# Scan of a Mamba layer: C rows through DRAM in fp32, C products shared by VectorE and GpSimd, one drive tile scaled on VectorE

## The reference, cut to what matters

```python
x_dbl = einsum('bld,ed->ble', silu(conv(x)), x_proj_w)   # 8 + 16 + 16 rows
dt = softplus(x_dbl[..., :8] @ dt_proj_w.T + dt_proj_b)
Bm, Cm = x_dbl[..., 8:24], x_dbl[..., 24:]
def step(h, inputs):                                     # over the tokens
    dA = exp(dt_t[..., None] * A)
    h = h * dA + (dt_t * x_t)[..., None] * B_t[:, None, :]
    y = einsum('bds,bs->bd', h, C_t)
y = (ys + D * x) * silu(z)
```

## Time and profile before

| | |
|---|---|
| device time, median of 3 runs | 2769.23 us (2762.33 to 2771.55) |
| profiled execution, span | 2740.5 us |
| profiled execution, own time | shown only as its span |
| VectorE busy | 2446.6 us, 89% |
| TensorE busy | 2368.5 us, 86% |
| ScalarE busy | 2302.2 us, 84% |
| GpSimd busy | 1461.6 us, 53% |
| DMA mean | 40 GB/s |

### The profile page before, as it was taken

One profiled execution on the slowest core, in us unless ns is written; L12 is line 12 of the kernel. 1 busy time (PEld: TensorE's weight loads), 2 busy tenths in 40 slices (PEclk: granted clock), 3 DMA queues, 4 the chain that ended last, 5 costly groups with the idle time before them and its releaser, 6 DMA issues.

```text
span 2740.5 us, 93631 instructions
## 1 busy us (share of the span) xinstructions
PE 2368.5 (86%) x38272; PEld 1254.1 (46%) x38289; DVE 2446.6 (89%) x3408; ACT 2302.2 (84%) x4212; POOL 1461.6 (53%) x2897
## 2 busy tenths in 40 slices
...
GB/s 137 1 0 1 23 77 113 63 49 62 34 39 29 49 54 42 31 37 48 48 43 26 49 43 53 36 33 49 34 56 32 42 47 33 40 29 11 2 1 16
DMA packets 47022, 110.41 MB, mean 40 GB/s; under 512 B 5250, under 2 KB 39938, under 8 KB 42306
## 3 DMA queue, kind: packets, MB, share of 16 engines
...
## 4 chain that ended last, share of the span: by engine, by line
PE 36%; issue 17%; DVE 12%; ACT 12%; POOL 11%; DMA 1%; ACTq 0%; DVEq 0%; SPq 0%; POOLq 0%
PE bank L709 11%; PE bank L778 11%; PE bank L789 9%; ACT E L1052 9%; DVE NM L1430 8%; POOL acc L1668 2%; POOL H L1678 1%; ACT acc L1003 1%; POOL H L1681 1%; POOL smp L1661 1%; PE bank L690 1%; POOL dg L1726 1%; PE bank L703 1%; ACT UB L1014 1%; POOL H L1684 1%
## 5 line engine op out<-in xcount | busy, mean ns | idle before, releaser
L1430 DVE TENSOR_REDUCE NM<-bank 128x1 f32<-128x1024 f32 x1536 | 1798.8, 1207 | 77.6 <-PE bank L778 56.8
L1052 ACT ACTIVATE E<-bank,NM 128x1024 f32<-128x1024 f32 x1536 | 1707.4, 1118 | 164.1 <-DVE NM L1430 138.1
L778 PE MATMUL bank<-KS,QS 72*32 72x512 bf16 x12288 | 960.0, 388 | 162.0 <-ACT E L1052 110.1
L789 PE MATMUL bank<-E,dg 128*32 128x256 f32 x12288 | 925.4, 385 | 1.7 <-ACT acc L1003 1.7
L1726 POOL TENSOR_TENSOR dg<-mask,RZ 128x128 f32<-128x128 f32 x384 | 153.0, 398 | 825.7 <-DVE RZ L1440 720.7
L778 PEld LDWEIGHTS bank<-KS,QS 72*32 72x32 bf16 x12288 | 252.4, 96 | 706.4 <-ACT E L1052 587.3
L789 PEld LDWEIGHTS bank<-E,dg 128*32 128x32 f32 x12288 | 385.0, 111 | 292.3 <-issue 62.6
L1052 ACT ACTIVATION_READ_ACCUMULATOR E<-bank,NM 128x1 f32 x1536 | 310.2, 202 | 0.0
L1668 POOL TENSOR_TENSOR acc<-acc,rel 128x256 f32<-128x256 f32 x384 | 272.3, 729 | 7.8 <-ACT acc L1003 7.8
L709 PE MATMUL bank<-H,ET 128*32 128x129 f32 x6144 | 189.5, 275 | 6.3 <-DVE ET L1373 6.3
L709 PE MATMUL bank<-hT,WL 128*32 128x256 f32 x2304 | 164.3, 389 | 26.2 <-ACT UB L1014 21.8
...
## 6 DMA issues: line engine op xcount, KB each, us to landing
...
```

What stands on the lines that cost most here:

```text
L778: inst = PE_.matmul(bank[x % 3][32 * i:32 * i + 32, k * 512:k * 512 + 512], QS[0:72, half % 2, 4 * hq + i, r0:r0 + 32], KS[0:72, b, k, 4 * ...
L789: inst = PE_.matmul(pb(6)[32 * k:32 * k + 32, 256 * grp:256 * grp + 256], dg[:, x // 4 % 3, x % 4, :], E[:, x % NE, :].rearrange("p (i k c ...
L1052: A_.activation(E[:, x % NE, :], bank[x % 3][:, :], ACT.Exp, bias=NM[:, x % 4:x % 4 + 1], accum_out=ZS[:, quad % 3, j:j + 1]).then_inc(s[" ...
L1430: V.tensor_reduce(NM[:, x % 4:x % 4 + 1], bank[x % 3][:, :], AX.X, ALU.max, negate=True).then_inc(s["rowmax"], 1)
```

## The change

C no longer goes through bf16 parts and TensorE. `xpc` makes C's 16 rows alone, ScalarE copies them to `CR` (`crow`), and SP stores them to DRAM (`crows`) and loads two states at a time back, each row to all 128 partitions, into `CB` with two buffers (`c_rows`). `sel`, `BC3`, `hi`, `rest`, `mid`, `low` and `spread` are gone. Of four steps, VectorE makes the products of the first two (state g even) and GpSimd those of the last two (`mulP`), at step p = n and directly ahead of its sum. VectorE scales the last of the drive's four token tiles, two steps ahead, and ScalarE three. The spare pieces of the scan use four banks (2 and 3 are free during it), always the one taken longest ago. SP's loads of expert weights and fill tables, which it issued together at the start, are issued one behind each load of C rows; the fill is cut in 16.

```diff
+CROWS = 2
...
-                15: "z0", 16: "z1", 17: "xpbc xpdt", 20: "btp dtp0", 21: "dtp1", 28: "utp0", 29: "utp1"},
-         "ACT": {6: "xt", 17: "silu0 silu1 silu2 silu3", 20: "hi dr", 22: "mid bt", 23: "abs0", 24: "abs1 exp", 27: "ln",
+                15: "z0", 16: "z1", 17: "xpc xpdt", 20: "btp dtp0", 21: "dtp1", 28: "utp0", 29: "utp1"},
+         "ACT": {6: "xt", 17: "silu0 silu1 silu2 silu3", 20: "crow dr", 22: "bt", 23: "abs0", 24: "abs1 exp", 27: "ln",
                  30: "ut0 ut1"},
-         "DVE": {-4: "bn", -3: "var", 0: "xn", 18: "rest", 20: "low", 22: "one", 25: "sum"},
+         "DVE": {-4: "bn", -3: "var", 0: "xn", 22: "one", 25: "sum"},
          "POOL": {-3: "pow", 0: "xa", 3: "res", 26: "u0", 27: "u1"}}
 DONE = {"PE": {14: "outp"}, "ACT": {}, "DVE": {4: "y2", 14: "x1"}, "POOL": {5: "yz0", 6: "yz1"}}
...
+def made(engine, n):
+    ours = (0, 1) if engine == "DVE" else (2, 3)
+    return n // 4 * 2 + sum(i <= n % 4 for i in ours)
+def product_of(n):
+    engine = "DVE" if n % 4 < 2 else "POOL"
+    return ("mulC" if engine == "DVE" else "mulP"), made(engine, n)
+def summed(n):
+    return n // 4 * 2 + n % 2 + 1
 def in_order(engine, k):
...
-    uses = [(k, x) for k, x in order if x in SPARE]
-    table = {}
-    for m, (k, x) in enumerate(uses):
-        wait = None
-        if m >= 2:
-            k0, x0 = uses[m - 2]
-            name, per, add = SPARE[x0]
-            wait = (name, per * k0 + add)
-        table[x, k] = (6 + m % 2, wait)
+    ready = [x for at in READY["PE"].values() for x in at.split()]
+    table, users = {}, {6: None, 7: None, 2: None, 3: None}
+    for k, x in order:
+        if x in SPARE:
+            at = [b for b in users if x in ready or b > 3][0]
+            table[x, k] = (at, users.pop(at))
+            name, per, add = SPARE[x]
+            users[at] = (name, per * k + add)
     return table
...
-                e.wait_ge(s["dbt"], 4 * g + 4)
+                e.wait_ge(s["dbt"], 3 * g + 3)
+                e.wait_ge(s["dbt_end"], g + 1)
...
-            def spread(g):
-                k, st_ = divmod(g, 16)
-                if st_ == 0:
-                    e.wait_ge(s["bc_low"], k + 1)
-                if g >= 2:
-                    e.wait_ge(s["mulC"], 2 * g - 2)
-                PE_.matmul(pb(2 + g % 2), sel[:, st_, :], BC3[:, toks(k)], start=True, stop=True).then_inc(s["spread"], 1)
...
-                e.wait_ge(s["two"], two(n) + 1)
+                e.wait_ge(s["two"], summed(n))
...
-                if 0 <= p - 7 < CSTEPS and p % 4 in (3, 0):
-                    ysum(p - 7)
-                if 0 <= p < CSTEPS and p % 2 == 0:
-                    spread(p // 2)
+                for late, at in ((6, 0), (7, 1)):
+                    if 0 <= p - late < CSTEPS and (p - late) % 4 == at:
+                        ysum(p - late)
...
-                        for t in range(4):
+                        for t in range(3):
                             A_.activation(dBT[:, g % 2, t, :], UT[:, k % 2, t, :], ACT.Copy, scale=BT[:, k % 2, t, st_:st_ + 1]).then_inc(s["dbt"], 1)
...
-                e.wait_ge(s["spread"], g + 1)
+                e.wait_ge(s[f"ld_c{g // 2 % CROWS}"], 16 * (g // 2 // CROWS + 1))
                 if n >= 8:
-                    e.wait_ge(s["y"], two(n - 8) + 1)
-                V.tensor_tensor(hC[:, n % 8, :], pb(2 + g % 2), hs[:, n % NH, :], ALU.mult).then_inc(s["mulC"], 1)
+                    e.wait_ge(s["y"], summed(n - 8))
+                V.tensor_tensor(hC[:, n % 8, :], CB[:, g // 2 % CROWS, g % 2, :], hs[:, n % NH, :], ALU.mult).then_inc(s["mulC"], 1)
...
-                        e.wait_ge(s["mulC"], p - NH + 1)
+                        name, count = product_of(p - NH)
+                        e.wait_ge(s[name], count)
...
-                if 0 <= p - 1 < CSTEPS:
+                if 0 <= p - 1 < CSTEPS and (p - 1) % 4 < 2:
                     mul_c(p - 1)
+                if 0 <= p + 2 < CSTEPS and p % 2 == 0:
+                    g = (p + 2) // 2
+                    k = g // 16
+                    if g % 16 == 0:
+                        e.wait_ge(s["ut"], 2 * k + 2)
+                        e.wait_ge(s["bt"], k + 1)
+                    if g >= 2:
+                        e.wait_ge(s["drive"], 2 * g - 2)
+                    V.tensor_scalar(dBT[:, g % 2, 3, :], UT[:, k % 2, 3, :], BT[:, k % 2, 3, g % 16:g % 16 + 1], None, ALU.mult).then_inc(s["dbt_end"], 1)
...
-                n = p - 2
+                n = p
                 if 0 <= n < CSTEPS and n % 4 >= 2:
-                    e.wait_ge(s["mulC"], n + 1)
+                    g = n // 2
+                    e.wait_ge(s["scan"], n + 1)
+                    e.wait_ge(s[f"ld_c{g // 2 % CROWS}"], 16 * (g // 2 // CROWS + 1))
+                    if n >= 8:
+                        e.wait_ge(s["y"], summed(n - 8))
+                    G.tensor_tensor(hC[:, n % 8, :], CB[:, g // 2 % CROWS, g % 2, :], hs[:, n % NH, :], ALU.mult).then_inc(s["mulP"], 1)
+                    e.wait_ge(s["mulP"], made("POOL", n))
+                    e.wait_ge(s["mulC"], made("DVE", n - 2))
                     G.tensor_tensor(hC[:, (n - 2) % 8, :], hC[:, (n - 2) % 8, :], hC[:, n % 8, :], ALU.add).then_inc(s["two"], 1)
...
+            def late_load(j):
+                if j == 1:
+                    e.dma_start(W1[:, :, :], io["moe_w1"].rearrange("e p w -> p e w")).then_inc(s["ld_moe"], 16)
+                elif j == 2:
+                    e.dma_start(W2[:, :, :, :], io["moe_w2"].rearrange("e (c p) d -> p (e c) d", p=128).rearrange("p (e c) d -> p e c d", c=2)).then_inc(s["ld_moe"], 16)
...
+                elif 8 <= j < 24:
+                    to, r = io[("first", "second")[j // 4 % 2]][j // 16], ROWS // 4 * (j % 4)
+                    e.dma_start(to[r:r + ROWS // 4, :], io["fill"][r:r + ROWS // 4, :]).then_inc(s["ld_fill"], 16)
+            def c_rows(k):
+                e.wait_ge(s["crow"], k + 1)
+                e.dma_start(io["crows"][k], CR[:, :]).then_inc(s["c_store"], 16)
+                e.wait_ge(s["c_store"], 16 * k + 16)
+                for j in range(8 * k, 8 * k + 8):
+                    if j >= CROWS:
+                        name, count = product_of(4 * (j - CROWS) + 3)
+                        e.wait_ge(s[name], count)
+                        name, count = product_of(4 * (j - CROWS) + 1)
+                        e.wait_ge(s[name], count)
+                    src = io["crows"][k, 2 * (j % 8):2 * (j % 8) + 2, :].unsqueeze(0).to_broadcast([128, 2, CH])
+                    e.dma_start(CB[:, j % CROWS, :, :], src).then_inc(s[f"ld_c{j % CROWS}"], 16)
+                    late_load(j)
...
+            for k in range(CHUNKS):
+                c_rows(k)
```

More of the change, by code:

```diff
@@ L96, in carried @@
     return p // 64 * 32 + p % 32 + 1
-def two(p):
-    return p // 4 * 2 + p % 2
+def made(engine, n):
[6 more added lines that the diff above has]
+    return n // 4 * 2 + n % 2 + 1
 def in_order(engine, k):
@@ L336, in build @@
         XS = sbuf(pa, "XS", [128, 2, T])
-        BC3 = sbuf(pa, "BC3", [128, T], BF16)
+        CB = sbuf(pa, "CB", [128, CROWS, 2, CH])
         DT = sbuf(pa, "DT", [128, 2, 2, CH])
@@ L898, in side_act @@
                 A_.activation(DR[:, :], pb(BANKS["xpdt", k][0])[0:8, :], ACT.Copy).then_inc(s["dr"], 1)
-            elif p == "mid":
-                e.wait_ge(s["bc_rest"], k + 1)
-                if k:
-                    e.wait_ge(s["bc_low"], k)
-                A_.activation(MB[:, :], rest[:, :], ACT.Copy).then_inc(s["bc_mid"], 1)
             elif p == "bt":
```

66 lines of the change are left out of this document (24 added, 42 removed).

## The result

The changed kernel took 2773.57 us (median of 20 runs, 2766.96 to 3043.01), the kernel before 2765.67 us beside it (20 runs, 2757.11 to 2771.55): ratio 1.0037, 95% interval 1.0026 to 1.0047. That is slower, by little more than a measurement can tell from no change. One run, at 3043.01 us, had a granted TensorE clock of 0.73, where the others had 0.94, and is left out of the ratio. The prediction was 2777 us.

What follows compares the result with a forecast made beforehand. The prediction took VectorE, busy 89% and near its limit in the scan, as the bound. Locks with VectorE's saving +8, GpSimd's load +16, banks -9 and -7, transfers 0 gave +8 us: 2777 us, range 2750 to 2806.

Steps and rivals of the forecast that it cites:

- 29 us outside the span: Time of the kernel before outside its profiled span (2740.5 against the 2769.23 us median), taken as unchanged.
- Part 1: VectorE's regular work in the scan: two of four products go, two scalings come; alone -18 us.
- Parts 2 and 3: VectorE and GpSimd locking each other out of SBUF, +8 us with VectorE's regular saving included; GpSimd's added load, +16 us.
- Part 4: Spare banks: shorter steps 15 to 18 in three chunks, -9 us together; shorter steps 46 and 78, -7 us.
- Part 5: Transfers of C rows, late weights and fill: loads land in 4.5 us, wanted 9 us later; cost 0.
- the lock hardly bites: Faster rival in the scan: VectorE asks first each time, so GpSimd hardly holds it; -30 us, 2739; chance 0.22.
- C rows late: Slower rival in the scan: loads of C land late, 1 us a group; +32 +8, 2809 us; chance 0.05.
- the banks save nothing: Slower rival at the spare pieces: the new banks give no gain; +24 us, 2793; chance 0.03.
- Queue of locks: Slower rival in the scan: every VectorE lock instruction waits 0.5 us for GpSimd, four times a group; +36, 2805; chance 0.28.

Runs made afterwards that it cites:

- e6: Changed kernel with GpSimd's products and sums cut to 8 of 512 columns, work left out; one run, 2734.04 us, scan 276.6 us.
- second and third profile: The changed kernel unaltered, profiled again on two other chips; 1.0051 and 1.0064 of the kernel before, scans 317.8 and 314.2 us.
- e4: Changed kernel without both moves between engines: C rows by transfers and new banks, all products on VectorE, all scaling on ScalarE; 0.9966 of the kernel before.
- e9: C rows by transfers with the old bank rule, all products on VectorE, all four tiles on ScalarE; 1.0020 of the kernel before.
- e7: Changed kernel with C rows' loads after the first two cut to 8 of 512 columns, work left out; one run, 2774.45 us.
- e5: Changed kernel with chunk 3's products on VectorE, GpSimd making its own only in steps under 96; 1.0032 of the kernel before.
- e8: Changed kernel with all four tiles scaled on ScalarE and no GpSimd products from step 112; 0.9978 of the kernel before.

## Why the prediction was right

The sum was +8 us; the medians give +8 in the first comparison and +12 and +15 in the two others, so that the first hit the number is luck. In the scan it was +17 (13 to 21), and the scan begins 1.8 to 2.2 us sooner, where I had half a microsecond at most: VectorE's first work on `E` of chunk 0 begins at 32.85 us in place of 34.70, with the split of B and C gone ahead of it. By steps:

- **The time outside the span.** "29 us outside the span" was wrong. The profiled run after has a span of 2779.3 us and an own time of 2781.15, 1.85 apart. The profile of before, at 2740.5, fits the 2745.25 of chip 1 and not the 2769.23 of the table. Since only differences were added, nothing came of it.
- **Part 1 (-18)** is the step that failed. The durations were right (product 0.66, scaling 0.32 for my 0.35), but that they shorten the group was not. With next to no hold (e6) a group takes 6.9 us with or without the carry, where I had 6.2 and 6.5. I had treated VectorE as the only bound of the regular half. Two scans in a row need two drives in 2.4 us, and TensorE gives the next one later, as the timeline of e6 shows for one group. Steps 4 to 14 of e6 take as long as before, together within 1 us, where I had -5.6. For parts 1 and 4 together e6 gives -24 where I had -34.
- **Parts 2 and 3 (26 of holds, 16 of load, together 42).** e6 takes both away and gives back 41 in its one run: as a sum, this was right. The trace has 31 us of holds on VectorE (scaling 25, product 6) and 11 us more than before on GpSimd. The groups came near the forecast, but in part for another reason, since the floor was 6.9 and not 6.2: in chunk 1 7.9 to 8.6 us in the second and third profile and up to 10.5 in the first (I had 7.7), in chunk 0 6.8 or 7.9, by the pattern (7.0). I had thought the product the first to be held; it is the scaling. And the 0.87 us of the held instruction of before is not quite the rest of the sum, which was 1.01.
- **Part 4 (-16).** Right in e4 against e9, which have neither scaling nor GpSimd products to hold VectorE: -17.6. In the changed kernel itself -7 to -14 by the ratio. At steps 46 and 78 it was -3.5 and -4.4 for a forecast of -3.5 each; at steps 15 to 18 -2.5 and -1.9 in chunks 0 and 1 for -2.7 each, and nothing in chunk 2 (9.55 for 8.89), where the routing lies between.
- **Part 5 (0)** held: landings in 3.8 us, and e7.
- **Missed: C out of PSUM.** All of VectorE's products become instructions that GpSimd can hold, +6 us by e9. In part 2 I counted the hold of the groups, so some of it is in the 42; its effect on the scatters, 2.1 us longer together, was in no part.
- **Missed: GpSimd's order in chunk 3.** I counted GpSimd's load there, and not what is queued behind its product. Steps 118 to 121 cost 6.4 to 6.9 us more than before; e5 and e8 give 5.8 and 5.2 back. Of this 3.5 us are there in e6 too; the rest is in the 42.

So the total was near with an error in part 1, too much gain in the regular half. By stretches, with part 1 spread as 0.56 us a group, e6 shows where it went. The chunk starts are 4.8 us shorter than before (I had 2.2), and steps 18 to 32 of chunks 0 to 2 8.8 us (I had 6), which makes up for the regular half. Steps 14 to 18, with the banks, give 13.9 us for some 17, and chunk 3 from step 18 on is 3.3 us longer where I had 2 shorter, 3.5 of it in steps 118 to 121. These two are most of the 10 us between -24 and -34, and so of the distance between +8 and +17. Of the rivals, *the lock hardly bites* is refuted by the scaling's mean of 0.715, *C rows late* by the landings, *the banks save nothing* by e9. *Queue of locks* is nearer than its 2805: it asked for four holds of 0.5 us in each group; the products are held 0.1 us on average, and the scaling lasts over 0.55 us in 24 to 28 of 64 cases.

What stays open: which of the two patterns of chunk 0 a run takes, and why; and how the 25 us of the scaling divide into waits of TensorE's drive and time that VectorE lacks.
